# Self-attention of a decoder layer: scores in float32 on four row groups of the array, with q, k and v kept on chip

## The reference

```python
q = x @ w_q.T;  k = x @ w_k.T;  v = x @ w_v.T          # then (B, S, 16, 16)
scores = jnp.einsum('bqhd,bkhd->bhqk', q, k) * scale   # scale = 16 ** -0.5
weights = jax.nn.softmax(scores, axis=-1)
out = jnp.einsum('bhqk,bkhd->bqhd', weights, v)
x = _layernorm(x + out.reshape(B, S, D) @ w_o.T)
x = _layernorm(x + cross_attention(x, ctx))            # unchanged by the diff
x = _layernorm(x + experts(x))                         # unchanged by the diff
```

## Time and profile before

| | us |
|---|---|
| median of 3 runs | 890.18 |
| lowest, highest | 890.01, 895.51 |
| the profiled execution | 897.14 |
| its span, first to last instruction | 895.4 |
| PE, DVE, ACT, POOL busy in that span | 688.3, 377.0, 322.3, 218.7 |

### The profile page before, as it was taken

How to read it: one execution, slowest core, us unless ns; L and a number is a source line. 1 busy time by engine, 2 the same in 40 slices (tenths; PEclk the granted TensorE clock), 3 DMA queues, 4 the chain that set the end, 5 groups by cost and what they waited for, 6 DMA issues and landing times.

```text
span 895.4 us, 13630 instructions
## 1 busy us (share of the span) xinstructions
PE 688.3 (77%) x4099; PEld 451.6 (50%) x4100; DVE 377.0 (42%) x789; ACT 322.3 (36%) x541; POOL 218.7 (24%) x265
## 2 busy tenths in 40 slices
PE   7562365999999986765677862099999999999980
PEld 3231111222222245542213652089999999999970
DVE  2251344988888446664444875001111111111114
ACT  2220133767676643333354212033333333333312
POOL 1021200111111122112111167223333344343322
PEclk9876786999999998886789985589999999999995
DMA  6999993000001431859835815312112112222105
GB/s 193 132 170 168 119 170 39 3 1 1 1 1 52 126 53 38 129 83 134 138 100 191 279 49 142 106 23 37 31 27 35 25 29 35 31 33 32 22 10 187
DMA packets 67346, 71.11 MB, mean 79 GB/s; under 512 B 14548, under 2 KB 60141, under 8 KB 67310
## 3 DMA queue, kind: packets, MB, share of 16 engines
q1 hardware_dynamic: 54574, 58.03, 33.8%
q0 software_dynamic: 8512, 8.44, 6.0%
q10 hardware_dynamic: 4224, 4.19, 1.6%
HBM read 50.45 MB, written 21.40 MB: 80 GB/s over the span
## 4 chain that ended last, share of the span: by engine, by line
PE 65%; DMA 14%; DVE 7%; SPq 4%; POOL 4%; issue 3%; ACT 2%; DVEq 0%; ACTq 0%; POOLq 0%
PE ps L1582 16%; PE ps L1593 15%; PE ps L1303 7%; PE ps L1312 7%; PE ps L1248 6%; DMA scrq<-parts 5%; DMA qst<-mT 5%; POOL metas L664 3%; PE ps L1396 3%; SPq L401 2%; PE ps L1469 2%; PE ps L1462 2%; DMA qst<-scr_q 1%; PE ps L1408 1%; PE ps L1428 1%
## 5 line engine op out<-in xcount | busy, mean ns | idle before, releaser
L898 DVE TENSOR_REDUCE nmx<-ps 128x1 f32<-128x512 f32 x256 | 160.2, 681 | 55.3 <-PE ps L1248 55.3
L745 ACT ACTIVATE probs<-ps 128x512 f32<-128x512 f32 x256 | 133.7, 607 | 94.0 <-PE ps L1303 93.7
L1582 PEld LDWEIGHTS ps<-xtT,w1c 128*128 128x128 f32 x1248 | 148.1, 195 | 4.3 <-DVE w1c L367 1.5
L1582 PE MATMUL ps<-xtT,w1c 128*128 128x128 f32 x1248 | 148.5, 278 | 1.8 <-DVE w1c L367 1.3
L1593 PE MATMUL ps<-wexp,hidT 128*128 x624 | 141.0, 379 | 0.0
L1303 PE MATMUL ps<-qst,kst 99*128 (+1 forms) x256 | 96.0, 395 | 34.9 <-DMA qst<-mT 32.9
L1593 PEld LDWEIGHTS ps<-wexp,hidT 128*128 128x128 f32 x624 | 115.7, 190 | 14.0
L1248 PE MATMUL ps<-kst,qst 96*128 (+1 forms) x256 | 94.1, 393 | 34.9 <-DMA kst<-scrk 17.5
L1209 DVE TENSOR_SCALAR yw<-ps,mt 128x256 f32<-128x256 f32 x39 | 18.9, 484 | 219.9 <-PE ps L1593 219.9
L851 ACT ACTIVATE hidT<-ps 128x1024 f32<-128x1024 f32 x39 | 39.9, 1023 | 195.8 <-PE ps L1582 190.9
L703 POOL DMA_INDIRECT acc<-yw,mt x39 | 68.0, 1742 | 165.8 <-DVE yw L1209 161.4
(11 more groups left out here) (165 smaller groups left out, 695.4 us busy)
## 6 DMA issues: line engine op xcount, KB each, us to landing
wexp<-in_w1T SPq DMA_DIRECT2D x8, 1024.0 KB
wexp<-in_w2T SPq DMA_DIRECT2D x8, 1024.0 KB
qst<-scrq SPq DMA_DIRECT2D x24, 256.0 KB, 9.8
kst<-scrk SPq DMA_DIRECT2D x24, 256.0 KB, 19.7
qst<-scr_q SPq DMA_DIRECT2D x24, 256.0 KB, 8.8
scrq<-parts SPq DMA_DIRECT2D x4, 768.0 KB, 18.6
scrk<-parts SPq DMA_DIRECT2D x4, 768.0 KB, 19.4
scr_q<-parts SPq DMA_DIRECT2D x4, 768.0 KB, 3.4
```

Of the source, the lines that this page charges most:

```text
L745: act.activation(probs[n % 8][:, :], ps[:, 4 + n % 3, :], ACT.Exp).then_inc(s_exp, 1)
L898: dve.tensor_reduce(nmx[j % 2][:, k:k + 1], ps[:, slot, :], AX.X, ALU.max, negate=True).then_inc(s_mfree, 1)
L1582: mm = pe.matmul(ps[:, 2 * (j % 2) + f // 4, f % 4 * P:(f % 4 + 1) * P], w1c[j % 2][:, k * FF + f * P:k * FF + (f + 1) * P], xtT[j % 2][:, ...
```

## The change

Stacks, splits and their trips through HBM go. PE projects q, k and v of a half batch (128 columns = 8 heads) into one bank. ACT copies q twice, with a scale by partition that is zero on half of the rows (`own_q`), and DVE copies k in the same way (`k_units`), so that `qm[u]` and `km[u]` hold the four heads of unit u in four groups of 32 partitions: 16 rows of data and 16 spare ones, of which one holds the negative maximum in `qm` and a one in `km`. Both stay in SBUF for all 16 units. A score tile is one float32 matmul with a depth of 32 rows, from the row group of its head. The columns of w_v are put in the order of the units (`wvu`), and ACT writes v right into `vu`.

The maxima are float32 too: `max_turn` is a float32 matmul by the identity, and four DMAs for each unit write the rows. Max tiles have banks 0 to 2, exp tiles 3 to 5, projections bank 6, pv bank 7. Max tiles run 26 tiles ahead (`LEAD`). pv of the group before stands behind the second exp tile of a group. The projections of batches 1 to 3 stand inside the loop, six for each batch, every eighth exp tile. All loops over units are unrolled on all engines. SP loads the remaining x, late weights and the residual one after the other behind the rows of each unit; x of batch 0 is loaded through ACT's queue. The rows of w_o are permuted with the heads. The diff, cut to its core:

```diff
+UNITS = NB * NU
+TILES = HG * QT
+LEAD = 26
+TURN_AT = 3
...
+    qm = [sb(f"qm{u}", S, F32, R_Q) for u in range(UNITS)]
+    km = [sb(f"km{u}", S, F32, R_Q) for u in range(UNITS)]
...
+    PROLOGUE = {1: 2, 3: 3, 6: 4, 9: 5}
+    PROJECTED_AT = {3 + 8 * n: n for n in range(6)}
+    def projection_at(e):
+        b, at = e // (NU * TILES) + 1, e % (NU * TILES) - 4
+        return (b, PROJECTED_AT[at]) if b < NB and at in PROJECTED_AT else None
...
     def _(sp):
-        def make_stacks(b):
-            for qk in range(2):
-                sp.wait_ge(s_p3, 2 * b + qk + 1)
-                sp.dma_start(scr[qk][ds(b, 1)]...).then_inc(s_st[qk], 16)
...
+        def max_rows(w):
+            sp.wait_ge(s_mfree, turn_slot(w) + 1)
+            r = max_row(w % 2)
+            for i in range(HG):
+                sp.dma_start(qm[w][2 * HD * i + r:2 * HD * i + r + 1, :].rearrange("p (a t) -> p a t", t=P),
+                             mT[w % 2][QT * i:QT * (i + 1), :]).then_inc(s_mrow[w % 2], 16)
...
+        for w in range(UNITS):
+            max_rows(w)
+            BEHIND_ROWS[w]()
...
     def _(pool):
+        pool.wait_ge(s_w[2], 16)
+        for k in range(KD):
+            for m in range(KD):
+                copy(wvu[...], wv_s[...]).then_inc(s_wvu, 1)
+        for i in range(2):
+            pool.memset(vu[i][:, :], 1.0).then_inc(s_vones, 1)
...
     def _(act):
+        def q_units(b, m):
+            act.wait_ge(s_proj, 6 * b + 2 * m + 1)
+            for j in range(2):
+                act.activation(qm[NU * b + 2 * m + j][:, :], ps[:, proj_bank(b, 2 * m), :], ACT.Identity,
+                               scale=own_q[:, j:j + 1]).then_inc(s_qev, 1)
...
+        act.wait_ge(s_own, 3)
+        act.wait_ge(s_vones, 2)
+        for n in range(6):
+            evict(0, n)
+        for e in range(UNITS * TILES):
+            act.wait_ge(s_e, e + 1)
+            if e % HG == 0 and e >= 8:
+                act.wait_ge(s_pv, e // HG - 1)
+            act.activation(probs[e % 8][:, :], ps[:, 3 + e % 3, :], ACT.Exp).then_inc(s_exp, 1)
+            if projection_at(e):
+                evict(*projection_at(e))
...
     def _(dve):
+        for e in range(UNITS * TILES):
+            maxima(e + LEAD)
+            if e % TILES == 1 and e >= TILES:
+                o_out(e // TILES - 1)
+            if projection_at(e) and projection_at(e)[1] in (1, 3):
+                k_units(projection_at(e)[0], projection_at(e)[1] // 2)
...
     def _(pe):
+        def max_tile(w, k):
+            n, (qt, i) = max_slot(w, k), divmod(k, HG)
+            if n >= 3:
+                pe.wait_ge(s_mfree, n - 2)
+            rows = slice(2 * HD * i, 2 * HD * (i + 1))
+            pe.matmul(ps[:, n % 3, :], qm[w][rows, qt * P:(qt + 1) * P], km[w][rows, :], start=True, stop=True).then_inc(s_mready, 1)
...
+        def exp_tile(e):
+            u, (kt, i) = e // TILES, divmod(e % TILES, HG)
+            if e % TILES == 0:
+                pe.wait_ge(s_mrow[u % 2], 16 * HG * (u // 2 + 1))
+            if e >= 3:
+                pe.wait_ge(s_exp, e - 2)
+            rows = slice(2 * HD * i, 2 * HD * (i + 1))
+            pe.matmul(ps[:, 3 + e % 3, :], km[u][rows, kt * P:(kt + 1) * P], qm[u][rows, :], start=True, stop=True).then_inc(s_e, 1)
+        def pv(g):
+            u, kt = divmod(g, QT)
+            if kt == 0:
+                pe.wait_ge(s_oev, u)
+            pe.wait_ge(s_exp, HG * (g + 1))
+            for i in range(HG):
+                mm = pe.matmul(ps[VW * i:VW * (i + 1), 7, :], vu[b % 2][:, at:at + VW], probs[g % 2 * HG + i][:, :],
+                               start=(kt == 0), stop=(kt == QT - 1))
...
+        for t in range(LEAD):
+            maxima(t)
+            if t in PROLOGUE:
+                project(0, PROLOGUE[t])
...
+        for e in range(UNITS * TILES):
+            exp_tile(e)
+            maxima(e + LEAD)
+            if e % HG == 1 and e >= HG:
+                pv(e // HG - 1)
+            if projection_at(e):
+                project(*projection_at(e))
+            if e == CONTEXT_V:
+                context_v()
+            if e == CONTEXT_K:
+                context_k()
```

More of the change, by code:

```diff
@@ L42 @@
 MROWS = ROWS + 3
-M3W = 96
 CAP = T // P
@@ L740, in exps @@
-        def exps(u):
-            for n in range(HG * QT):
-                act.wait_ge(s_e, HG * QT * u + n + 1)
-                if n % HG == 0 and not (isinstance(u, int) and 4 * u + n // HG < 2):
-                    act.wait_ge(s_pv, 4 * u + n // HG - 1)
-                act.activation(probs[n % 8][:, :], ps[:, 4 + n % 3, :], ACT.Exp).then_inc(s_exp, 1)
-        act.wait_ge(s_proj, 3 * NB)
-        exps(0)
-        with act.Fori(1, NB * NU) as u:
-            exps(u)
+        act.dma_start(xTb[0][:, :].rearrange("p (k n) -> p k n", k=KD),
+                      xT.rearrange("(k p) n -> p k n", p=P)[:, :, 0:S]).then_inc(s_xT[0], 16)
@@ new lines, in maxima, with k_units @@
+        def maxima(t):
+            w, k = divmod(t, TILES)
+            if w < UNITS:
+                row_max(w, k)
+            if w > 0 and k == TURN_AT - 1 and w < UNITS:
+                max_T(w - 1)
+            if t == UNITS * TILES - 1:
+                max_T(w)
+        def k_units(b, m):
+            dve.wait_ge(s_proj, 6 * b + 2 * m + 2)
+            for j in range(2):
+                dve.tensor_scalar(km[NU * b + 2 * m + j][:, :], ps[:, proj_bank(b, 2 * m + 1), :], own[:, j:j + 1],
+                                  spare_row[:, 1 - j:2 - j], ALU.mult, ALU.add).then_inc(s_kev, 1)
@@ L1364, in context_k @@
             mm.then_inc(s_c, 1)
[L1366 to L1371 removed]
+        project(0, 0)
+        project(0, 1)
+        pe.wait_ge(s_ident, 3)
+        for t in range(LEAD):
+            maxima(t)
+            if t in PROLOGUE:
+                project(0, PROLOGUE[t])
+        pe.wait_ge(s_qev, NU)
+        pe.wait_ge(s_kev, NU)
+        pe.wait_ge(s_vev, 2)
+        for e in range(UNITS * TILES):
[5 more added lines that the diff above has]
+                project(*projection_at(e))
+            if e == CONTEXT_V:
+                context_v()
+            if e == CONTEXT_K:
+                context_k()
+        pv(UNITS * QT - 1)
+        pe.wait_ge(s_oev, UNITS)
         def turn_o(ph, n):
```

466 lines of the change are left out of this document (164 added, 302 removed).

## The result

Before: 890.1 us (median of 4, 888.16 to 895.51). After: 909.21 us (median of 4, 905.07 to 912.96). The ratio is 1.021, with a 95% interval of 1.0154 to 1.0267: the change makes the kernel slower, by 2.1% (between 1.5 and 2.7%), where 1.6% faster was forecast. The profiled execution of the kernel after took 910.04 us, its span 908.1.

The account below looks back on a forecast made before the run. Bound by a front waiting for bf16 stacks through HBM, then the attention loop. Attention's end: 36 + 248.2 + 18 + 5.5 + 5.5 = 313.2 against 327.1 us, so 890.2 - 13.9 = 876 us; range 848 to 945.

Parts of the forecast that it names:

- two-wide rival: Loop: halves of neighbouring tiles keep program order, so only two tiles overlap; 5.05 us a group, 950 us; chance 0.13.
- serial rival: Loop: tiles don't share the array at all; 8 us a group, 1130 us; chance 0.05.
- a latency loop: New loop: waits from pv to pv set the group's 3.86 us, with ACT needing 1.9 and DVE 2.4.
- The term: Plain group of four exp and four max tiles, pv to pv: 3.86 us, 62 groups making 239.3.
- M5 follows E5: Group's last max tile (M5) after its last exp tile (E5): +0.07 us, its bank freed by a reduction, not an exp.
- 15 turns of the maxima, +0.37 each: Loop: each turn, a float32 matmul into another tile shape, costs drain and changeovers; 5.5 us in all.
- leaves E4, M4, E5, M5 as one wave: Loop groups with a projection: the last two exp and two max tiles run together; +1.0 us each, 18 us.
- First max tile 13.7: Front: first max tile at 13.7 us, after ACT's wait for POOL's copies and memsets until 13.0.
- Ten max tiles with four projections: 24.8: Front: ten max tiles and four projections (4 x 1.71 + drains) done at 24.8 us.
- The clock: Loop rival: quarter-filled tiles might not hold the fast clock; 6.4 us a group, 1030 us; chance 0.04.
- waves cost more: Loop rival: eight float32 weight loads of 128 columns a wave; 4.15 to 4.6 us a group, 894 to 922; chance 0.17.
- My 0.45 for faster: Whole kernel: chance 0.45 of below 881 us; front gives 77.7, loop takes back 63.8, 13.9 us earlier.

Follow-up runs that it names:

- one_group: Kernel after with every score tile reading rows 0 to 31, so all lie on one row group; 1645.95 us.
- bf16_pairs: bf16_four_banks with max tiles in two pairs, behind the first exp tile and ahead of pv, and projections behind a pv; 904.47 us, ratio 1.0091.
- half_evict: Kernel after with exps and reductions handling only 256 of 512 columns, matmuls unchanged; 891.23 us (one run).
- bf16_max: front_act with max tiles made from bfloat16 copies of q and k, banks still three and three; 887.18 us, ratio 0.9931.
- four_exp_banks: front_act with the six score banks shared four to exp tiles and two to max tiles; 945.19 us, ratio 1.0576.
- turn_at_pv: Kernel after with TURN_AT 4 instead of 3, the turn of the maxima right in front of pv; 900.32 us, ratio 1.0103.
- front_act: turn_at_pv with ScalarE loading its table early and waiting for GpSimd's vu fills only ahead of the first v units; 893.52 us, ratio 0.9998.
- bf16_max_first: bf16_pairs with the first max pair ahead of the exp tile and projections back behind the fourth exp tile; 883.5 us, ratio 0.9865.
- k_on_scalar: bf16_max_first with the copies of k of batches 1 to 3 made by ScalarE instead of VectorE; 875.68 us, ratio 0.9801.
- bf16_four_banks: bf16_max and four_exp_banks together: bfloat16 max tiles in two banks, float32 exp tiles in four; 906.87 us, ratio 1.0127.

## Why the prediction was wrong

**Right: what bounds the kernel before, and the sharing.** The bf16 stacks' hole disappears with the stacks. Four row-group tiles start together (0.03 us), so the two-wide and the serial rival fall; one_group shows what serial would have cost, 15.8 us a group at the lower clock. The Trainium skill's rule that matmuls keep program order in start and end ("TensorE: Matmul & The Clock Gate", The mechanism), weighed in the prediction, holds for whole tiles and not for their halves. The trace of after has the four tiles at 257.01, 257.02, 257.03 and 257.04 and their second halves at 257.55 to 257.57, in the order of the program; but the second half of the first tile starts behind the first half of the fourth. Since halves do not wait for each other in this way, the two-wide rival falls. For the signals it holds too: in bf16_pairs that of a short tile came no sooner than that of the long one ahead of it.

**Right: a latency loop.** The runs half_evict, bf16_max and four_exp_banks show it from three sides. The term was 0.13 us too small: M5 follows E5 by 0.14 and not 0.07, a first half in an empty array takes 0.53 and not 0.48, and the exp is 0.03 later. A short M5 takes the 0.14 off again (3.86 in bf16_max). 36 groups: 4.8 us.

**Wrong: "15 turns of the maxima, +0.37 each".** The step costed the turn and the projection each by itself. Nine of the 15 turns stand one tile behind a projection and cut the wave that the prediction counted on ("leaves E4, M4, E5, M5 as one wave"). 1.37 us each instead of 0.37, with the projection's own 0.2: 10.7 us; six turns alone were 0.36 short and one group stood longer: 2.5. The positions were in the code: e % 16 = 7 for projections, the max tile behind e % 16 = 8 for the turn. turn_at_pv shows it: one constant takes 12.7 us off the loop, and no group of 6.42 is left.

**Wrong: the front, by 11.5 us.** Three terms failed. (1) "First max tile 13.7" left out ScalarE's table load of 1.28 us behind the wait for GpSimd: 14.47, although GpSimd was done at 12.3 and not 13.0. That is 0.8 us. (2) The tiles. "Ten max tiles with four projections: 24.8" allowed 11.1 us; front_act, with projections at full speed, has them from 13.16 to 25.56, 12.4. For the sixteen tiles and the turn behind them, up to the first exp tile, the sum allowed 36 - 24.8 = 11.2; front_act takes 38.63 - 25.56 = 13.1, with a wait of 0.77 and one of 0.28 for a reduction and its last 6.6 us at the lower clock. That is 1.3 + 1.9 = 3.2 us. (3) The clock. I wrote that quarter-filled tiles might not hold it and gave that 0.04, for the loop, and against it that TensorE would never be idle. It was the front where it happened. The ten tiles and four projections took 15.7 us in after (14.47 to 30.18), 3.3 more than in front_act, with the projections at 2.93 and 3.39 us instead of 1.98; from 30.18 to the first exp tile 14.2 us against 13.1; and from there to the first pv 6.9 against the 3.8 forecast, with halves of 1.06 us. Together 0.8 + 3.2 + 3.3 + 1.1 + 3.1 = 11.5.

**Rival and range.** The time, 909.2, lies in the range of 848 to 945 and in the price range of the rival "waves cost more" (894 to 922), but that rival's mechanism, dearer waves in every group, accounts for 4.8 us of 31. Some two thirds (22.2 us) were collisions and the front, which no rival had: all of them varied the plain group or the clock in it. My 0.45 for faster rested on a margin of 14 us that was the difference of two large numbers (77.7 and 63.8), with a front costed by summing durations at full clock.

**What stays open.** Why the clock is lower in the front at all while max tiles, but for one turn, run alone: the records cover 9.72 of 10 us (34 to 44 us of after) on four row groups, as in the loop, where 1.00 is granted. Why the runs differ in the front's later slow stretch: front_act and half_evict reach their first exp tile at 38.63 and 39.06 us, with clocks of 0.80 and 0.82 from 20 to 40, although half_evict's first max tile starts no earlier (14.44) than that of after. In half_evict the reductions are shorter as well, so this does not tell the idle time and the waits apart. The front also differs where nothing was edited to change it: the first exp tile of turn_at_pv is at 46.32 us and that of after at 44.41, one profiled execution each, so a part of these differences may belong to the execution. No run held the clock up in the front on purpose. Nor is it settled what, beside 1.9 us, separates bf16_max_first from k_on_scalar.

## What to carry to other kernels

Where full-height instructions (turns, projections) interrupt a stream of row-group tiles, write down the position of each within the period before costing them, and put them where the array drains anyway; a cost per kind misses collisions. In a loop that is a chain of hand-overs, look for the ring that ends the wait last and count its banks, and put the short instruction ahead of the long one when another engine waits for it. Cost a front at both levels of the clock when it holds tiles that fill a part of the array or follows an idle time.

## What the runs showed of the hardware

- TensorE without a pause but with every score tile on the same 32 of 128 rows was granted 0.50 to 0.59 in every 20 us from 80 to 980 us (one_group); the same tiles spread over the four row groups were granted 1.00 in the loop of after, but 0.50 from 34 to 44 us, where max tiles, but for one turn, run alone.
- After 2.28 to 3.62 us of idle time (five executions) the first projection behind it, mostly both, ran at the lower clock; after 0.99 or 1.00 us (eight executions) neither did.
- Four float32 tiles of 32 x 128 by 512 columns in four row groups: second halves 0.53 us behind the first in an empty array, 1.16 us to the first exp. Neighbours on the same row group instead: 0.82 us more in a group of eight.
- The signal of a bfloat16 tile issued behind a float32 tile of another row group came 0.80 us after the end of its own record, with that of the float32 tile; issued ahead of it, 0.04 us after.
- An instruction at the head of TensorE's queue that waits for a bank holds up a tile behind it that needs nothing (0.69 us in bf16_four_banks).
- The table load of ScalarE took 1.28 us, inside the critical front.
